# Another order for the setup batch of a fused attention and ternary-FFN kernel: which engine ternarises which weight chunk, and when

## The reference, cut to what matters

```python
x = x + tanh(g_xattn) * attention(layernorm(x), ctx, ctx)   # 16 heads; a first softmax gives per-head
                                                            # features, an MLP turns them into a
                                                            # temperature, a second softmax is the real one
x = x + tanh(g_ffn) * ffn(layernorm(x), w1, w2)             # w1: 2048x512, w2: 512x2048

def _quant_weight(w):                  # per matrix, one scale for all of it
    s  = clip(mean(abs(w)), 1e-5)
    wq = clip(round(w / s), -1, 1) * s
```

## Time and profile before

| | |
|---|---|
| median of three executions | 1380.33 us |
| the profiled execution's own time | 1382.32 us |
| its span in the trace | 1380.5 us |
| `body(-1)`, to the first row of stage A on VectorE | 0 to about 65.4 us |
| `body(0)`, to the first scores of the second softmax | about 65.4 to 194.4 us |
| all that follows | 1186.1 us |

### The profile page before, as it was taken

One profiled execution on the slowest core, in us unless ns is written; L12 is line 12 of the kernel. 1 busy time (PEld: TensorE's weight loads), 2 busy tenths in 40 slices (PEclk: granted clock), 3 DMA queues, 4 the chain that ended last, 5 costly groups with the idle time before them and its releaser, 6 DMA issues.

```text
span 1380.5 us, 23490 instructions
## 1 busy us (share of the span) xinstructions
PE 1193.1 (86%) x6684; PEld 440.3 (32%) x6684; DVE 1103.3 (80%) x2054; ACT 922.7 (67%) x1527; POOL 421.9 (31%) x399
## 2 busy tenths in 40 slices
PE   5736669999989899999999999999999999869958
PEld 2202321344214431344224432344224431233224
DVE  6298779988798969897898969897898879983246
ACT  4463579756885769765985669664985679636713
POOL 4279474520253124510253124510353101100210
PEclk9857879999999999999999999999999999979979
DMA  8710221122112221012212221112112210001000
GB/s 295 227 51 11 62 68 38 36 46 62 61 48 47 47 71 54 22 28 62 62 47 47 47 79 47 28 32 58 55 47 46 55 54 1 1 1 62 1 0 31
DMA packets 35473, 73.70 MB, mean 53 GB/s; under 512 B 7952, under 2 KB 7952, under 8 KB 34832
## 3 DMA queue, kind: packets, MB, share of 16 engines
q1 hardware_dynamic: 35344, 72.13, 18.2%
HBM read 38.39 MB, written 8.39 MB: 34 GB/s over the span
## 4 chain that ended last, share of the span: by engine, by line
PE 50%; DVE 27%; issue 10%; ACT 8%; POOL 1%; SPq 1%; DMA 1%; DVEq 1%; ACTq 0%; POOLq 0%
PE b_ps L1274 11%; DVE stat L930 7%; PE o_ps L1485 6%; DVE nmax L925 5%; PE o_ps L1274 5%; PE o_ps L1314 4%; PE z_ps L1274 4%; ACT region L755 4%; PE a_ps L1295 4%; PE b_ps L1301 4%; ACT etile L738 3%; DVE hmax L1079 2%; PE z_ps L1485 2%; PE b_ps L1450 2%; PE z_ps L1325 2%
## 5 line engine op out<-in xcount | busy, mean ns | idle before, releaser
L738 ACT ACTIVATE etile<-a_ps,nmax 128x512 f32<-128x512 f32 x512 | 368.2, 731 | 141.9 <-DVE nmax L925 141.6
L755 ACT ACTIVATE region<-b_ps,inv2t 128x512 f32<-128x512 f32 x512 | 353.3, 754 | 50.0 <-PE b_ps L1301 45.9
L925 DVE TENSOR_REDUCE nmax<-a_ps 128x1 f32<-128x512 f32 x512 | 345.7, 677 | 41.7 <-PE a_ps L1295 37.9
L930 DVE BATCH_NORM_STATS2 stat<-etile 128x6 f32<-128x512 f32 x512 | 347.8, 682 | 12.7 <-ACT etile L738 12.3
L1295 PE MATMUL a_ps<-kst,qst 96*128 96x512 f16 x512 | 202.8, 401 | 60.8 <-ACT etile L738 49.8
L1301 PE MATMUL b_ps<-qst,kst 97*128 97x512 f16 x512 | 192.6, 388 | 20.5 <-DVE region L1102 7.7
L1314 PE MATMUL o_ps<-region,vbuf 128*32 128x512 f32 x1024 | 137.9, 606 | 13.0 <-ACT region L755 7.0
L1325 PE MATMUL z_ps<-region,ones 128*32 128x512 f32 x1024 | 136.2, 604 | 8.4 <-DVE region L950 8.4
L1301 PEld LDWEIGHTS b_ps<-qst,kst 97*128 97x128 f16 x512 | 49.1, 96 | 290.2 <-ACT region L755 258.3
L655 POOL TENSOR_TENSOR region<-region 128x512 f16<-128x512 f32 x64 | 76.0, 1188 | 203.9 <-ACT region L788 203.7
L611 POOL TENSOR_TENSOR region<-region 128x512 f32<-128x512 f32 x32 | 40.8, 1276 | 292.0 <-DVE region L957 292.0
(11 more groups left out here) (280 smaller groups left out, 1981.0 us busy)
## 6 DMA issues: line engine op xcount, KB each, us to landing
kst<-region SPq DMA_DIRECT2D x96, 128.0 KB, 2.3
qst<-region SPq DMA_DIRECT2D x96, 128.0 KB, 2.3
xres<-in_x_dram SPq DMA_DIRECT2D x8, 1024.0 KB, 5.7
out_dram<-xres SPq DMA_DIRECT2D x32, 256.0 KB, 2.1
cin<-in_ctxT_dram SPq DMA_DIRECT2D x30, 256.0 KB, 2.7
cin<-in_x_dram SPq DMA_DIRECT2D x28, 256.0 KB, 2.6
kst<-in_f1T_dram SPq DMA_DIRECT2D x2, 1024.0 KB, 12.0
qst<-in_f2T_dram SPq DMA_DIRECT2D x2, 1024.0 KB, 10.8
```

What stands on the lines that cost most here:

```text
L738: nc.scalar.activation(etile[:, k % E_SLOTS, :], a_ps[k % A_BANKS][:, :], ACT.Exp, bias=nmax[:, slot_of(n), t:t + 1], scale=1.0).then_inc( ...
L755: nc.scalar.activation(probs[:, (s + 1) % 2, g, :], b_ps[g % 2][:, :], ACT.Exp, scale=inv2t[:, slot:slot + 1]).then_inc(b_exp, 1)
L925: vec.tensor_reduce(nmax[:, slot_of(k // T), k % T:k % T + 1], a_ps[k % A_BANKS][:, :], AX.X, ALU.max, negate=True).then_inc(a_max, 1)
L930: vec.bn_stats(stat[:, slot_of(k // T) * T + k % T, :], etile[:, k % E_SLOTS, :]).then_inc(a_stat, 1)
```

## The change

In `body(0)`:

- GpSimd splits all four context chunks at once, and no ternary chunk stands between or behind them. It has two ternary chunks instead of three, and late: chunk 3 between the split of x and the low halves of Q, chunk 2 at its end.
- VectorE has six chunks: 0, 1, 6, 7, 4, 5. Each takes one of its instructions instead of two. The other half of the work is done by ScalarE, whose `sign` writes the sign of w + s/2 (function Sign with a bias); VectorE then writes the minimum of that and (w > s/2).
- The magnitudes are summed in another order (w1 is complete after the sixth chunk), at sets 0, 2, 4, 6, 8, 10. The sum, TensorE's addition and the scale stand in three separate places of the streams, three sets apart from the first to the last.
- Stage A has 16 tiles in the 16 sets instead of 28, and 4 tiles beside each of the 12 products instead of 3; a product's 12 matmuls come in pieces of 3 instead of 4 between the tiles.
- Chunk 7 is loaded into `region4` and not into the space of chunk 2, so its load waits for the last Q product of `body(-1)` and not for a ternary chunk. The first two context chunks of batch 1 are loaded ahead of the five weight chunks.

In `body(-1)`: the two gates are loaded ahead of Wq, and their tanh stands behind the second weight split on ScalarE, no longer behind the last V product. VectorE waits for that tanh ahead of stage A, before and after.

The diff, cut to its core; its hunks are, in this order, the tables, SyncE, GpSimd (two), ScalarE (three) and VectorE (three).

```diff
-A_PLAN_0 = (28, (3, 3, 3, 3, 0, 0, 0, 0, 3, 3, 3, 3, 3, 3, 3, 3))
+A_PLAN_0 = (16, (4, 4, 4, 4, 0, 0, 0, 0, 4, 4, 4, 4, 4, 4, 4, 4))
...
-MAGNITUDES_AT = {0: 2, 1: 3, 2: 6, 3: 4, 5: 5, 9: 7}
-SCALES_AT = {4: 0, 11: 1}
-TERNARY_AT = {5: 2, 7: 3, 13: 6, 14: 4, 15: 5}
-POOL_CHUNKS, DVE_CHUNKS = (0, 1, 7), (2, 3, 6, 4, 5)
+MAGNITUDE_ORDER = (0, 1, 6, 4, 2, 3, 5, 7)
+MAGNITUDES_AT = {0: 6, 2: 4, 4: 2, 6: 3, 8: 5, 10: 7}
+SUMS_AT, TOTALS_AT, SCALES_AT = {8: 0, 12: 1}, {10: 0, 14: 1}, {11: 0, 15: 1}
+SIGNS_AT, SIGNS_BESIDE = {12: 0, 14: 1}, {0: 6, 1: 7, 2: 4, 3: 5}
+TERNARY_AT, TERNARY_BESIDE = {13: 0, 15: 1}, {1: 6, 2: 7, 3: 4, 2 * C: 5}
+POOL_CHUNKS, DVE_CHUNKS = (3, 2), (0, 1, 6, 7, 4, 5)
...
-                    for n in (2, 3, 4):
-                        load_f(n)
                     load_c(1, 0)
                     load_c(1, 1)
-                    load_f(5)
-                    load_f(7)
+                    for n in (4, 2, 3, 5, 7):
+                        load_f(n)
                     load_c(1, 2)
                     load_c(1, 3)
...
                     for c in range(C):
                         split_c(i + 1, c)
-                        if second and c % 2 == 1:
-                            make_ternary(c // 2)
...
+                if second:
+                    make_ternary(3)
...
                 if second:
-                    make_ternary(7)
+                    make_ternary(2)
...
+            act_waits.wait_ge(gate_in, 32)
+            nc.scalar.activation(tg[:, :], gates[:, :], ACT.Tanh).then_inc(setup_tanh, 1)
+
+            def sign(n):
+
+                k = n // 4
+                dst = f1[:, n, :] if n < 4 else f2[:, 4 * (n - 4):4 * (n - 3), :].rearrange("p k n -> p (k n)")
+                act_waits.wait_ge(f_sum, 2 * k + 2)
+                nc.scalar.activation(dst, f_from[n], ACT.Sign, bias=whalf[:, 1, k:k + 1], scale=1.0,
+                                     saturate=False) \
+                    .then_inc(tern_sign, 1)
...
+                    if isinstance(i, int) and i == 0 and s in SIGNS_AT:
+                        sign(SIGNS_AT[s])
...
+                    if isinstance(i, int) and i == 0 and n in SIGNS_BESIDE:
+                        sign(SIGNS_BESIDE[n])
                     if has_p:
                         qk_out(n, "K")
...
+            def ternary_sum(k):
+                dve_waits.wait_ge(f_abs, 1 + max(MAGNITUDE_ORDER.index(n) for n in range(4 * k, 4 * k + 4)))
+                vec.tensor_reduce(wsum[:, k:k + 1], wabs[:, k, :], AX.X, ALU.add).then_inc(f_sum, 1)
...
-                dve_waits.wait_ge(f_sum, 2 * k + 2)
-                vec.tensor_scalar(dst, w, whalf[:, 0, k:k + 1], None, ALU.is_lt, saturate=False).then_inc(f_below, 1)
-                dve_waits.wait_ge(f_below, order + 1)
+                dve_waits.wait_ge(tern_sign, DVE_CHUNKS.index(n) + 1)
                 vec.scalar_tensor_tensor(out=dst, in0=w, scalar=whalf[:, 1, k:k + 1], in1=dst,
-                                         op0=ALU.is_gt, op1=ALU.subtract, saturate=False).then_inc(tern_dve, 1)
+                                         op0=ALU.is_gt, op1=ALU.min, saturate=False).then_inc(tern_dve, 1)
...
-                    if second and n % 2 == 0:
+                    if second and n in TERNARY_BESIDE:
+                        make_ternary(TERNARY_BESIDE[n])
+                    if second and n % 2 == 1:
                         stat_x(1, n // 2)
```

47 lines of the change are left out of this document (25 added, 22 removed).

## The result

The changed kernel takes 1375.01 us (median of 8, 1373.00 to 1377.63); the kernel before, run beside it, 1381.78 (1379.63 to 1384.31). The ratio is 0.9950, its 95% interval 0.9938 to 0.9962: about 6.8 us won where 14.0 were forecast. The profiled execution took 1375.14 us (span 1373.3), that of before 1382.32 (1380.5).

What follows compares the result with a forecast made beforehand. VectorE was taken to set the pace of body(0): tile 63's maximum would start at 166.3 instead of 180.6, 14.3 earlier, less 0.3 for hand-overs, so 1380.3 - 14.0 = 1366.3 us; eight-in-ten range 1361.5 to 1373.

Steps and rivals of the forecast that it cites:

- Start: Before stage A: ScalarE is free of the last V output at about 65.1 us and begins its first magnitude.
- `body(-1)`: ... I cost this at 0, at most 0.4: Gate loads ahead of Wq shift its issue by about 1.5 us; cost taken as 0, at most 0.4 us.
- the early maxima: VectorE's first three maxima, 1.8 us of work, move to some 57 to 62 us but earn nothing by themselves.
- Sets, sign, K: body(0): magnitudes end at 83.4 us, a sign takes 1.9, the sets end at 92.8, K at 122.6.
- stall beside K: Beside K product 0: ScalarE's 5.4 us against VectorE's 4.8 make the next statistics wait some 0.9 us.
- The wait for x: At the second x statistics: x is loaded by 118.7 us, VectorE asks at 121.1, so all 9.39 us goes.
- The margin of 2.4: Slack in us between x's load ending (118.7) and VectorE's request for it (121.1).
- V and Q: Last parts of stage A: V ends at 144.0 us, transposes at 148.4, tile 63's maximum starts at 166.3.
- the 4.41: VectorE's wait in us behind the transposes of x, after V; forecast to stay.
- Beside V and Q it must be 2.4 GHz: TensorE must run at the high clock there to keep VectorE's 4.8 us beat for four tiles; taken as met.
- rival (c): TensorE at 1.2 GHz beside V and Q: one or two products, 1368 to 1370 (0.10); six or more (0.02).
- All behind it keeps its distance: Everything after tile 63's maximum, the 13.78 us tail and the 1186 us behind it, stays the same length.

Runs made afterwards that it cites:

- gates_late: Changed kernel with the gate loads back behind Wo and their tanh early, behind the split of Wo on ScalarE; 1374.85 us.
- gates_only: Kernel before with only the gates' move (loads ahead of Wq, tanh behind the second weight split); 1382.72 us.
- pool_early: Changed kernel with GpSimd's chunk 3 moved forward, behind the four context splits instead of behind the split of x; 1376.77 us.
- the warm kernels: Versions with 48 unread matmuls in TensorE's pause before body(0)'s second softmax, on the kernel before or the changed kernel with gates put back; 1364.51 to 1379.33 us.
- warm: Changed kernel with gate loads and tanh put back, plus 48 unread matmuls in TensorE's pause before body(0)'s second softmax; 1366.20 us.
- before_warm: Kernel before with 48 unread matmuls in TensorE's pause before the second softmax of body(0); 1379.33 us.
- warm_delay: warm with two small unneeded loads on SyncE's queue ahead of mrow in body(0); 1370.73 us.
- pairs: Changed kernel with only the sign undone, VectorE making each of its six chunks by two instructions again; 1378.01 us.
- the delays: Two unneeded loads ahead of mrow in body(0): 1382.79 us on the kernel before, 1374.56 on the changed kernel with gates put back, 1370.73 on warm.

## Why the prediction was wrong

The forecast was 1366.3 (range 1361.5 to 1373.0); the median was 1375.01, outside. Of the 8.7 us between them 1.5 are the base: the kernel before, run beside it, took 1381.78 and not 1380.33. Its direction was right, and its account of `body(0)` was right nearly row by row; two steps outside failed.

- **Start, and "`body(-1)`: ... I cost this at 0, at most 0.4"**: wrong, it costs 2.2 (1.8 in the two profiles of before and changed). I read that the loads ahead of Wq were still arriving and took Wq's own issue as slack. The two gate loads took 2.9 us on the queue and moved Wq's issue by 3.0, not by 1.5, and the split of Wq had already been waiting 7.16 us for its data: it was the next link, so nothing hid a delay. That the early maxima earn nothing was right (gates_late, gates_only).
- **Sets, sign, K**: taken from ScalarE's first magnitude, the steps fit. First sign 18.3 us behind it forecast, 18.19 measured; sign 1.9, measured 1.90 from start to start (85.19 to 87.09; the row's own duration is 2.07); stall beside K 0.9 and 0.90; second x statistics 56.0 and 55.93. The trace agrees with the Trainium skill here ("ScalarE: Activation LUTs", "Step-by-step: what each stage is for"): an element costs the same in Sign as in Abs.
- **The wait for x**: gone, as forecast. The margin of 2.4 was smaller. In pool_early the load was issued 2.1 us later (the row of two at 119.84 instead of 117.72) and 0.63 of wait came at a request 0.8 later than in the changed kernel, so the margin was about 2.1 - 0.6 - 0.8 = 0.7. The rest went where GpSimd works beside a chunk of VectorE: in the changed kernel the first of its two casts of x took 2.12 us, the second 0.61.
- **V and Q**: the 4.41 was 4.16. "Beside V and Q it must be 2.4 GHz" held beside V from 129.9 us on; before that, from 123.1, V's first products ran at 0.50 and no wait for scores came of it. Behind the transposes the clock was 0.50 from 146.9 to 153.8 and cost two waits of 0.4. That is rival (c) in its small form. The 0.8 more and the 0.25 less are nearly the 0.65 us by which the path (101.85) exceeds the forecast's 101.2.
- **"All behind it keeps its distance"**: wrong, and the larger error. In the profiles 4.5 of the 14 were lost there. The tail is indeed the same 13.8 us, but the 1186 us behind it are not a constant: they contain TensorE at two rates. In the kernel before TensorE came out of its pause, ran 5.4 us at 0.50, and met no fall from there to the end of `body(6)`. I had the time at 0.50 in my own table (0.98 over the whole stretch) and treated it as fixed. In the changed kernel's first profile the start of `body(1)` is no slower (5.3 us); the 4.5 are the three falls behind it. In the other profiles with the change 6.1 to 8.4 us at 0.50 follow the start of the second softmax (the warm kernels aside), and every profile had falls later.

What is shown: in the first profile the three bodies that are longer are those in which the clock fell; the pause ahead of `body(1)` causes the low clock at its start (warm, before_warm, warm_delay), which costs 1.1 us there in the old order and 1.5 in warm_delay; and with the pause filled the times of the two orders differ by the full gain of `body(0)`. What is settled in part: why the profiles with the change meet more falls (in all of them, against one of four without it). 19 of their 35 falls stand at TensorE's longer wait ahead of a sum of the second softmax. For the other 16, at the border of two batches, the wait is the same in all kernels, and it stays open why 15 of them came in the eight sign kernels without the idle matmuls, one in pairs and none in the three with them; the delays, which should have moved them, showed no rule. Nor is it explained why the warm kernels' bodies 2 to 6 (before_warm's too) are 3 to 4 us shorter than the 768.4 of the old order (the mean of the first row) and half of their time at 0.50 would give.

The page on TensorE's clock in the Trainium skill ("TensorE: Matmul & The Clock Gate", "HAM oscillation — how this bites in real kernels") names pauses between bursts as what puts a burst at half rate. I weighed it at the transposes, where it costs 0.8 us, and not at the pause of 16 us ahead of `body(1)`, in which TensorE has only the MLP's few matmuls, nor at the shorter ones behind it. At the long pause the runs agree with the rule: the clock is 0.50 behind it, and 1.00 once it is filled.

## What to carry to other kernels

When a stage is shortened, don't carry the distance to the end over as a constant: look at the granted clock at the border where the next TensorE-bound stage begins, and price the us at 1.2 GHz (here half a us each over all profiles, some 0.2 at the start of `body(1)`). A pause of TensorE that hands over to a TensorE-bound stage can be worth filling with matmuls that nobody reads; 48 of them won as much in the changed order as the whole change (6.8 us), and 1.7 in the kernel before. And look for rows behind the changed code whose wait has grown: 0.35 us more of one wait was where over half of the falls came. A load put ahead of others in a queue delays all of them, and the question to ask is whether an engine was already waiting for the one behind it.
